# Router logits with the gate weights stationary: four column tiles, the exponential ahead of a transpose

## The reference, cut to what matters

```python
# per token: d = 128 features, E = 16 experts, K = 4 chosen, H = 64 hidden per expert
g = sigmoid(xf @ gate_w.T)                     # router: [tokens, 16]
topv, topi = top_k(g, K)
wn = topv / sum(topv)                          # weights of the four chosen experts
combine = zeros_like(g).at[tokens, topi].add(wn)
h = silu(xf @ e_win[e]) * (xf @ e_vin[e]) * combine[:, e]
routed = sum over e of h @ e_wout[e]
shared = silu(xf @ ws_in) * (xf @ vs_in) @ ws_out
x = layernorm(xf + shared + routed)
```

## Time and profile before

| what | value |
|---|---|
| runs of the kernel before | 864.02, 866.17 (median), 871.2 us |
| the profiled execution | 864.57 us, span 862.8 us |
| TensorE matmul busy | 91% of the span, 5783 instructions |
| VectorE busy | 75% |
| ScalarE busy | 42% |
| GpSimd busy | 43% |
| granted TensorE clock, mean | 0.963 |
| first expert layer to last (176.6 to 822.6 us) | 15 groups of 42.1 to 43.9 us |

### The profile page before, as it was taken

How to read it: one execution, slowest core, us unless ns; L and a number is a source line. 1 busy time by engine, 2 the same in 40 slices (tenths; PEclk the granted TensorE clock), 3 DMA queues, 4 the chain that set the end, 5 groups by cost and what they waited for, 6 DMA issues and landing times.

```text
span 862.8 us, 17647 instructions
## 1 busy us (share of the span) xinstructions
PE 787.7 (91%) x5783; PEld 666.1 (77%) x5783; DVE 644.4 (75%) x1711; ACT 363.7 (42%) x621; POOL 371.7 (43%) x370
## 2 busy tenths in 40 slices
PE   6888968689999999999999999999999999999976
PEld 5656656578888888888888798888898888888855
DVE  5799953377778777777777877777878777778754
ACT  4757833143434343434343434343434343434131
POOL 5050008553455455454545544545455454543200
PEclk8999977599999999999999999999999999999979
DMA  4887744030404040404040405040404040400000
GB/s 121 237 259 262 288 177 127 30 123 25 135 24 134 24 134 24 134 24 134 24 132 26 134 24 132 26 133 25 134 24 134 24 134 24 134 24 25 1 13 13
DMA packets 53104, 81.01 MB, mean 94 GB/s; under 512 B 10176, under 2 KB 36952, under 8 KB 49112
## 3 DMA queue, kind: packets, MB, share of 16 engines
q1 hardware_dynamic: 53080, 80.68, 30.4%
HBM read 55.24 MB, written 25.43 MB: 93 GB/s over the span
## 4 chain that ended last, share of the span: by engine, by line
PE 45%; DVE 19%; issue 15%; DMA 9%; POOL 6%; ACT 2%; SPq 2%; POOLq 1%; DVEq 1%; ACTq 0%
PE bank L1395 11%; DMA max_b<-max_scratch 8%; PE bank L1366 5%; PE bank L1370 5%; PE bank L1367 5%; DVE acc L838 5%; PE bank L1339 3%; DVE st L990 3%; PE bank L1315 3%; PE bank L1385 3%; PE bank L1313 2%; PE bank L1320 2%; DVE Y L1002 2%; POOL D L548 2%; POOL D L538 2%
## 5 line engine op out<-in xcount | busy, mean ns | idle before, releaser
L754 ACT ACTIVATE s_in<-bank 128x512 f32<-128x512 f32 x144 | 86.1, 598 | 175.9 <-PE bank L1370 174.8
L1395 PEld LDWEIGHTS bank<-ewout,h 128*128 128x128 f32 x1024 | 132.8, 191 | 8.5
L1366 PE MATMUL bank<-yT_hi,in_hi 128*128 128x512 f32 x288 | 128.0, 444 | 8.3 <-DVE h L1097 8.3
L1395 PE MATMUL bank<-ewout,h 128*128 128x128 f32 x1024 | 134.9, 275 | 0.0
L1097 DVE TENSOR_TENSOR h<-s_in,bank 128x512 f32<-128x512 f32 x144 | 98.2, 682 | 49.0 <-PE bank L1370 42.2
L552 POOL TENSOR_TENSOR rs<-ve,half 128x4 f32<-128x4 f32 x32 | 32.6, 1019 | 206.6 <-DVE ve L998 206.6
L1370 PE MATMUL bank<-yT_lo,in_hi 128*128 128x512 f32 x288 | 114.3, 397 | 0.0
L1367 PE MATMUL bank<-yT_hi,in_lo 128*128 128x512 f32 x288 | 113.9, 395 | 0.0
L538 POOL TENSOR_TENSOR D<-a_tok,max_b 128x512 f32<-128x512 f32 x64 | 65.4, 1043 | 110.7 <-DVE max_b L910 67.8
L1101 DVE TENSOR_TENSOR h<-h,bank 128x512 f32<-128x512 f32 x128 | 87.2, 681 | 14.4 <-PE bank L1385 14.4
L951 DVE TENSOR_TENSOR state<-kept,bank 64x130 f32<-64x130 f32 x128 | 36.6, 286 | 59.1 <-PE bank L1320 29.6
(11 more groups left out here) (193 smaller groups left out, 1623.6 us busy)
## 6 DMA issues: line engine op xcount, KB each, us to landing
xact_scratch<-xact SPq DMA_DIRECT2D x16, 1024.0 KB, 4.8
max_b<-max_scratch SPq DMA_DIRECT2D x15, 1024.0 KB, 7.8
xa<-xact_scratch SPq DMA_DIRECT2D x16, 512.0 KB, 6.2
silu_z<-xact_scratch SPq DMA_DIRECT2D x16, 512.0 KB, 3.8
inter_w<-inter_scratch SPq DMA_DIRECT2D x30, 256.0 KB, 7.1
x_in<-in_L_attn_x_dram SPq DMA_DIRECT2D x16, 256.0 KB, 4.8
xt_scratch<-x_t SPq DMA_DIRECT2D x16, 256.0 KB, 4.9
xT<-xt_scratch SPq DMA_DIRECT2D x16, 256.0 KB, 8.2
```

Source lines behind the costliest of these rows:

```text
L754: act.activation(s_in[:, j % 2], bank[4][:], ACT.Silu).then_inc(silu_done, 1)
L1366: pe.matmul(o, in_hi[:, m, j], yT_hi[:], start=True, stop=False)
L1395: i = pe.matmul(bank[7][:, k * P:(k + 1) * P], h2[:, j % 2, k * P:(k + 1) * P], w, start=(j == k == 0), stop=(j == NJ), skip_group_check=True)
```

## The change

The logits are computed the other way around: the gate weights, padded with zeros from 16 to 32 columns, are stationary and the transposed tokens of a chunk (128 x 128) move; chunk k writes partitions 32k to 32k+31 of the bank, so the four products lie in four column tiles of the array. The exponential then runs on a 128 x 128 tile, expert rows on partitions (64 of the 128 hold logits, the others the zeros of the padding). TensorE transposes this `ge` back to tokens on partitions with one instruction (`gate_tokens`), placed behind the products of slot 0, and VectorE reads the transposed tile from PSUM when it adds 1. `routing` part 0 moves behind VectorE's product of slot 0. GpSimd clears w_gate in the setup with one more memset, and ScalarE waits for the transpose of the group before ahead of the exponential; TensorE's wait for `ge` ahead of `combine_transposes` goes.

```diff
@@ -97,7 +97,7 @@
         gate_rows = sb("gate_rows", [NX, P])
-        w_gate = sb("w_gate", [P, NX])
+        w_gate = sb("w_gate", [P, 2 * NX])
         w_down = sb("w_down", [P, NP, E])
@@ -246,7 +246,7 @@
         yT_lo = sb("yT_lo", [P, G], F32R)
-        ge = sb("ge", [P, NC, NX])
+        ge = sb("ge", [NC * 2 * NX, P])
         ge1 = sb("ge1", [P, NC, NX])
@@ -486,7 +486,8 @@
             pool.memset(g_pad[:], 0.0).then_inc(pool_const, 1)
-            pool.wait_ge(pool_const, 6)
+            pool.memset(w_gate[:], 0.0).then_inc(pool_const, 1)
+            pool.wait_ge(pool_const, 7)
             pool.affine_select(out=ident[:], in_=ident[:], compare_op=ALU.not_equal, fill=1.0, base=0,
@@ -681,7 +682,7 @@
                 copy(g_v[:].rearrange("p s d -> p (s d)"), small[:, n8:2 * n8])
-                copy(w_gate[:], small[:, 2 * n8:2 * n8 + NX]).then_inc(fold1_out, 1)
+                copy(w_gate[:, 0:NX], small[:, 2 * n8:2 * n8 + NX]).then_inc(fold1_out, 1)
             def fold_products():
@@ -740,8 +741,8 @@
                 act.wait_ge(logit_mm, f + 1)
-                act.activation(ge[:].rearrange("p k e -> p (k e)"), bank[6][:, 0:NC * NX], ACT.Exp,
-                               scale=-1.0).then_inc(ge_done, 1)
+                prev(act, ge_mm, f)
+                act.activation(ge[:], bank[6][:, 0:P], ACT.Exp, scale=-1.0).then_inc(ge_done, 1)
             def ffn_slot(f, j):
@@ -1019,8 +1020,6 @@
                 weigh_keys(g, 0)
-                if f is not None:
-                    routing(f, 0)
                 for j in range(NJ + 2):
@@ -1051,8 +1050,9 @@
                 if part == 0:
-                    dve.wait_ge(ge_done, f + 1)
-                    dve.tensor_scalar(ge1[:], ge[:], 1.0, None, ALU.add).then_inc(route, 1)
+                    dve.wait_ge(ge_mm, f + 1)
+                    dve.tensor_scalar(ge1[:], bank[6][:, 0:P].rearrange("p (k e) -> p k e", k=NC)[:, :, 0:NX], 1.0, None,
+                                      ALU.add).then_inc(route, 1)
                     after(1)
@@ -1112,10 +1112,10 @@
             def ffn(f):
-                routing(f, 0)
                 for j in range(NJ + 2):
...
                     if j == 0:
+                        routing(f, 0)
                         routing(f, 1)
@@ -1351,8 +1351,13 @@
                 for k in range(NC):
-                    i = pe.matmul(bank[6][:, k * NX:(k + 1) * NX], yT[:, k * P:(k + 1) * P], w_gate[:], start=True, stop=True)
+                    i = pe.matmul(bank[6][k * 2 * NX:(k + 1) * 2 * NX, 0:P], w_gate[:], yT[:, k * P:(k + 1) * P],
+                                  start=True, stop=True)
                 i.then_inc(logit_mm, 1)
+
+            def gate_tokens(f):
+                pe.wait_ge(ge_done, f + 1)
+                pe.transpose(bank[6][:, 0:P], ge[:], ident[:]).then_inc(ge_mm, 1)
             def ffn_in(f, j):
@@ -1371,7 +1376,6 @@
                 pe.wait_ge(route, (f + 1) * ROUTE)
-                pe.wait_ge(ge_done, f + 1)
                 for k in range(NC):
@@ -1402,6 +1406,8 @@
                     ffn_in(f, j)
+                if j == 0:
+                    gate_tokens(f)
                 if 2 <= j <= NJ + 1:
@@ -1482,12 +1488,12 @@
            6: (("H", None),), 8: (("D", 0),), 9: (("D", 1),)}
-DVE_SLOT = {0: (("route", 1), ("S", 0), ("route", 2)), 1: (("S", 1), ("route", 3), ("C", 1), ("K", 1)), 2: (("S", 2), ("R", 0)),
+DVE_SLOT = {0: (("route", 0), ("route", 1), ("S", 0), ("route", 2)), 1: (("S", 1), ("route", 3), ("C", 1), ("K", 1)), 2: (("S", 2), ("R", 0)),
             3: (("S", 3),), 4: (("R", 1),), 6: (("H", None),)}
 U_SLOT = {0: 0, 1: 1, 2: 2, 3: 3}
-IDENT = 7
-CONSTS = 12
+IDENT = 8
+CONSTS = 13
 SCAN_DECAY = 10
```

More of the change, by code:

```diff
@@ L299, in mixer_moe_block @@
         yT_hi_done, yT_lo_done = sem("yT_hi_done"), sem("yT_lo_done")
-        logit_mm, ge_done = sem("logit_mm"), sem("ge_done")
+        logit_mm, ge_done, ge_mm = sem("logit_mm"), sem("ge_done"), sem("ge_mm")
         route = sem("route")
@@ L498, in _ @@
                                base=-DH, pattern=[[0, DH]], channel_multiplier=1).then_inc(pool_const, 1)
-            pool.wait_ge(pool_const, 10)
+            pool.wait_ge(pool_const, 11)
             pool.affine_select(out=bm, in_=bm, compare_op=ALU.is_ge, fill=0.0, base=QD - 1,
```

## The result

The changed kernel takes 872.76 us (median of 20 runs, 868.3 to 877.44), the kernel before 867.04 us (median of 20, 861.29 to 874.61). The recorded ratio is 1.0094, 95% interval 1.0073 to 1.0114, which is some 8 us. It is not the quotient of the two medians: these lie 5.7 us apart (1.0066), and the two means 5.5 us, with an interval of 3.6 to 7.4 us worked out from the same 20 and 20 runs. Ratios leave out runs more than 1.5% above the fastest of their kernel, which matters most for the change with S0 early, where four of twelve runs go, among them the profiled one. The forecast was 867.5 us, 0.2% above its own base of 866.17 us, with 0.80 on a move within 1% and a range that reached to 874. The time lies in the range.

A forecast was written before the change was run, and what follows sets the result against it. VectorE's queue was taken to bound six groups, max_b's load nine. 6 x 0.22 = +1.3 us plus 0.1 us at the end gave +1.4 us: 866.0 us on the profiled execution, 867.5 us on the median; range 860.5 to 874.

The forecast's parts named there:

- What bounds the kernel: VectorE's queue, through state update S0, bounds the start of six groups; the load of max_b holds nine.
- early groups: Six of 15 groups with an expert layer, where max_b's load lands early; 42.11 us long, cost 0.22 us each.
- late ones: Nine groups whose chain of waits passes through the load of max_b; 43.38 us long, change costs 0.
- TensorE's steps: Logits hold TensorE about 0.48 us instead of 0.92; transpose adds 0.13 us; net worth nothing, ending in S0's wait.
- 0.25 us taken for slot 0: First products on TensorE start sooner after the logits, so slot 0 ends 0.25 us earlier (bounds 0 and 0.44).
- 0.10 and 0.22 us estimated for the two changes: TensorE's cost of changing into the column tiles (0.10 us) and out of them (0.22 us), around the logits.
- ScalarE: Exponential starts at 265.57 instead of 266.12 and takes 0.05 us more; silu behind it ends 0.5 us earlier.
- 0.22 us later: VectorE's maximum ends at 269.17 instead of 268.95, as product h goes first; delays state update S0 and chunk 1.
- stated bounds of 0 and 0.70 us: Limits on VectorE's delay: 0 if it stays gapless, 0.70 us if silu comes no earlier than before.
- The number that pay: Six groups whose max_b load lands early pay 0.22 us each, +1.3 us; the nine others pay 0.
- one of its six: The six groups whose max_b load lands early, each predicted to lengthen by 0.22 us.
- The second rival: VectorE's routing delayed 0.70 us runs comb2's last half into GpSimd's D: 875.6 us, slower by 1.1%; chance 0.08.

The follow-up runs named there:

- the change with S0 early: Changed kernel with state update S0 moved ahead of the search for the maxima: ratio 1.0009 (0.997 to 1.0048), median of all twelve runs 870.21 us.
- the delay alone: Kernel before plus one VectorE instruction (128x512, result unused) ahead of state update S0: ratio 1.0031, and on another chip 1.0089.

## Why the prediction was wrong

**What bounds the kernel** was read rightly: early groups are held by VectorE's queue through S0, late ones by the landing. The direction and the path of the cost were right too; what failed is the size of one term. In late groups of both kernels a group lasts as long as the load from issue to D's start plus 35.3 us (before: 8.67 and 43.94 us; after: 8.60 and 43.97 us), so there the change costs nothing, as said. In the profiled executions of the kernel before, of the changed kernel (two) and of the one with VectorE's order undone, the rule "the longer of the floor and this sum" gives the total of the 13 middle groups to 0.1 us, but for the groups in which comb2 meets D; with the delay alone the constant is 35.2 us. The floor is what a group lasts when its load is early.

**TensorE's steps** were right where they can be read. The logits' eight matmuls take 0.42 us (0.43 predicted), the transpose 0.11 us (0.13). Of the 0.25 us taken for slot 0 the trace gives less: chunk 0 starts 2.36 us behind the logits, before 2.39 (the third product waits for yT_lo); it was worth nothing either way. By the Trainium skill's rule, TensorEngine Tiling (Array Packing), Tiling Modes, a change of mode drains the engine. The 0.48 us to the next start looks like the 0.48 us predicted, but this is chance: it ends with ScalarE's yT_hi, so the rows of the changed loop neither show the 0.10 and 0.22 us estimated for the two changes nor speak against them.

**ScalarE** was right: exponential 0.28 us long and 0.73 us behind yT_hi's start (0.28 and 0.7 predicted), silu's end 2.76 us behind the logits (2.74).

**The step that failed is VectorE's, "0.22 us later".** By its own parts: h at 2.79 us behind the logits (2.78 predicted), the add at 3.39 (3.35), the reciprocal 0.25 us behind it (0.22; the add now reads PSUM and takes 0.22 us, not 0.18), and then the maximum 0.84 us behind the reciprocal, where 0.58 was predicted. The open wait was priced at 0.03 us and is 0.28 us. Together S0 is 0.56 us late, inside the stated bounds of 0 and 0.70 us, but two and a half times the value taken.

Half of the error in this wait could have been read from the trace of before. The 0.03 us is the wait between two instructions through a semaphore alone. Ahead of the maximum stands also the increment `alone(dve)`, and the other place that has it reads, in the group at 263.68:

```profile
269.66 0.09 DVE L1069 MATCH_VALUE_LOAD rest<-top,gext 128x8 f32 x1 [0.15 <-DVE top L1065]
```

So 0.15 us was there to be taken. The other 0.13 us could not be. It is not the length of the reciprocal: in the changed kernel the same two instructions have 0.52 us between them in the first overlapped group, 0.28 us in the 13 that follow in the loop, and 0.15 us in the last overlapped group, which is written out behind the loop:

```profile
795.51 0.18 DVE L1062 MAX8 top<-gext 128x8 f32<-128x20 f32 x1 [0.15 <-DVE gext L1057]
```

The kernels with the change or with its order on VectorE alone repeat these three values to 0.01 us. Why the loop adds 0.13 us, and its first pass 0.37 us, no run shows.

**The number that pay was too low as well.** A group pays if its landing does not already make it longer. Where 42.11 us was the floor it is now 42.74 us. With the 182 landings of all profiled executions, the rule "the longer of the floor and landing plus 35.3 us" gives 1.8 us for the 13 groups that wait for the load, the collisions of comb2 with D 1.0 us more (early landings under 5.75 us, 12% of all, no longer gain anything), the first group cost 0.9 us (44.17 against 43.28 us), the last 0.4 us: 4.1 us. The prediction counted the first as one of its six, at 0.22 us; with the 0.52 us wait S0 is 0.85 us late there.

**The second rival was partly what happened.** It had the place (comb2 in D), the mechanism, and the point from 0.34 us of delay on; it was held unlikely because the delay was thought to be 0.22 us. In the middle groups it happens once in an execution of the changed kernel, in both that were profiled, and in one and three groups of the two with the delay alone, not in six.

**What stays open.** The account gives 4.1 us. The measurement gives 8 us by the recorded ratio (6.3 to 9.9) and 5.5 us by the means (3.6 to 7.4), and the second measurement of the change 8 us by both. The delay alone gave 2.7 and 7.7 us by the ratios, 0.3 and 6.0 us by the medians. That the cost comes with VectorE's order is shown: undone, it is 1.0003 (0.9973 to 1.0032), and that order alone, on the kernel before, costs 1.1%. Its full size is not accounted for. As the rule fits each profiled execution, what is missing has to lie in where the landings fall, in how often comb2 meets D, or outside the groups; a slightly later mean landing behind a late S0 is the rival that no run tested. The two profiled executions differ by 10 us, mostly by their landings (mean to D's start 7.49 against 8.20 us), which is one draw each and no explanation for 20 runs each.

## What to carry to other kernels

An instruction between a producer and its reader on one engine can be doing work in the schedule: moving it away opens the wait it covered. To price that wait, look for a row in which everything that the program has between the two, the sequencer's own steps included, stands as it will stand; here it was 0.15 us and not 0.03, and even so came out at 0.28. Ask of a reordering not only when the moved step ends but when the last thing queued behind it begins, here a state update that TensorE and GpSimd wait for. And where a wait for a load decides part of the loop, moving the reader behind what does not need the load was worth more than the matmul change: 1.3% for two lines.

## What the runs showed of the hardware

On VectorE, an instruction that waits through a semaphore for the one directly ahead starts 0.03 to 0.04 us behind its end (the add and the reciprocal, in all kernels). With a semaphore increment of the sequencer's own between the two it is 0.15 us, behind a memset of 0.07 us and behind a reciprocal of 0.55 us alike; the latter pair has 0.28 us inside the hardware loop and 0.52 us in its first pass. VectorE's writes of comb2 from SBUF take 0.62 us beside GpSimd's scaling of the state and 0.7 to 1.1 us beside its D, against 0.20 to 0.23 us alone, while its products of 128 x 512 that read PSUM take 0.68 or 0.69 us with the same D beside them, no more than without it. And one load of 1 MB, issued 1.0 us behind the same other load, took from 4.6 to 9.4 us to land, from group to group.
